# Moving one 512-token group of the shared expert across the routed-expert stage, and summing five output tiles on another engine

## The chip, the cores and the metric

The kernel runs on one core of a Trainium2 chip. The metric is device time in microseconds (us) of one execution; less is better. Five engines work side by side, each through its own list of instructions in the order in which they are written: TensorE (PE in the profile; PEld is its weight loading), VectorE (DVE), ScalarE (ACT), GpSimd (POOL) and SyncE (SP), which here issues most of the transfers. They wait for each other through semaphores. SBUF is the on-chip memory, PSUM the eight banks (128 partitions x 512 floats) that TensorE writes its results to.

## What is computed

An attention-like block, then a mixture of experts with a shared expert, over 4096 tokens of 256 numbers in float32. The part that matters here:

```
xf = layernorm(x)                                  # 4096 tokens x 256
weights, indices = top_k(softmax(xf @ Wg), 4)      # 4 of 32 experts for each token
y = sum over the 4 experts e of a token:  (silu(xg @ W1[e]) * (xg @ W3[e])) @ W2[e] * weight
z = (silu(xf @ Ws1) * (xf @ Ws3)) @ Ws2            # the shared expert, 256 wide inside
out = x + y + z
```

## The kernel before

The 4096 tokens are 32 output tiles of 128 tokens (`NT`), and for the shared expert 8 groups of 512 (`NG`), four tiles each (`QT`). The work stands in four stages.

**Attention and routing** (to about 205 us). A loop `pipelined(NT, 7, step)` per tile; at its end the normalised tokens stand transposed in `x2T_all`, and POOL has written each token's row four times, once for each of its experts, to the table `xs` in HBM (L471).

**The first shared groups** (to about 255 us). For a group g, `shared_half(g, m, n)` (L740 to L746) multiplies one half m of the shared weights, n = 0 for Ws1 and n = 1 for Ws3, into one PSUM bank `h_bank(g, m, n)`: two multiplications of 128x512. `half_silu(g, m)` (ACT, L628) writes silu of the n = 0 bank to `sg`, `half_gate(g, m)` (DVE, L1237) multiplies it with the n = 1 bank to `gsh`, and `shared_z(g)` (L753 to L760) makes from `gsh` the group's four tiles of z in turn in the banks pQV and pO, each of which `add_z(t)` (DVE, L1247) adds to the output tile `xall[:, t]`. A tile's multiplication waits until the `add_z` two tiles earlier is through. Groups 0 to 2 (`NPRE = 3`) are made here, while the last rows of `xs` are written.

**The expert stage** (about 256 to 508 us). 144 blocks of table rows (`NJ`), 128 of one expert and 16 "mixed" ones of two halves. SP loads a block (L389, L394) into one of eight `xg` buffers; `expert_step` on PE transposes it into pT0 or pQV (L947), multiplies with W1 and W3 into pS0 or pS1 (L960 to L965), transposes the gated result into pT1 or pO (L952, L970) and multiplies with W2 into pS2 or pS3 (L978 to L981). ACT copies the transposed block (L649), takes silu (L653) and writes the weighted result (L661, L666); DVE gates and copies (L1342, L1346, and L1350 for the second halves of mixed blocks); POOL scatters the result to `ys` in HBM (L499), one row for each token and expert. The blocks are staggered: in one step PE transposes block i, multiplies block i-1 and so on, and a mixed block's later parts come a step later.

**The closing stage** (508 us to the end). Once all scatters have landed, SP loads for each output tile t its four parts (128 x 4 x 256, 512 KB, L402 and L405) into one of 24 buffers `parts(t)`, the first 24 at once, the others as buffers come free, and then stores the finished tiles (L412), two at a time and the last four alone. For each tile POOL adds parts 2 and 3 to parts 0 and 1 (one 128x512 addition in SBUF, L504); ACT copies the 512 sums to a PSUM bank (`copy_parts`, L676); DVE adds the two halves to `xall[:, t]` (`add_parts`, L1258 and L1260, one operand in SBUF and one in PSUM). Beside that, the shared groups 3 to 7 are made: PE makes group g's four halves, then the z of group g-1. The order on ACT and DVE is written out by hand, tile by tile (from L694 on ACT, from `half_gate(3, 0)` on DVE): for instance `half_gate(5, 1)` stands behind `add_parts(10)`, and `add_z(12)` behind `add_parts(2)` and `half_gate(4, 1)`.

What the steps below call a half is one call of `shared_half`; the profile shows each of its two multiplications as two rows, four in all.

## Time and profile before

| | us |
|---|---|
| median of 3 runs | 570.58 (570.04 to 571.71) |
| profiled execution, its own time | 570.52 |
| its span, first to last instruction | 568.8 |
| attention and routing | 0 to 205 |
| first shared groups | 205 to 255 |
| expert stage | 256 to 508 |
| closing stage | 508 to 568.8 |

| engine | busy, share of the span |
|---|---|
| PE | 540.5 us, 95% |
| ACT | 367.4 us, 65% |
| DVE | 360.4 us, 63% |
| POOL | 331.8 us, 58% |

All times in the profile are counted from the start of the span. A busy share is a mean over stages with different limits: in the closing stage PE, POOL and the transfers are all nearly always busy, and it is the order of the waits that tells which of them the others wait for.

### The profile page before, as it was taken

Reading aid. Unit: us, or ns where it says so; the run is one execution under the profiler, and the core shown is the slowest. Engines: PE = TensorE matmul, PEld = TensorE weight load, DVE = VectorE, ACT = ScalarE, POOL = GpSimd, SP = SyncE. Lnnn points to the kernel's source line nnn. Section 1 sums busy time; section 2 is a strip of 40 time slices with the busy share of each in tenths; the row PEclk is TensorE's granted clock in tenths of the full one; section 3 lists DMA queues with packets and bytes.
Section 4 is the critical chain, followed back from the end, with each engine's and each line's share of the span. In section 5 each row is a group of like instructions: output and inputs, shape, how many; then the busy total and the mean of one; then the engine's idle time right before and its main releaser. Section 6 shows DMA issues by size and latency. Waiting matters only on the chain.

```text
span 568.8 us, 17659 instructions
## 1 busy us (share of the span) xinstructions
PE 540.5 (95%) x4793; PEld 375.6 (66%) x4793; DVE 360.4 (63%) x1353; ACT 367.4 (65%) x1258; POOL 331.8 (58%) x367
## 2 busy tenths in 40 slices
PE   6899999999999998798999999999999999979996
PEld 3465666666666664366888888888888885534554
DVE  7698999999999994751333333333333336843886
ACT  3687999898999974303666666666666665643452
POOL 6010477677777777751655565565566564447991
PEclk8999999999999999797999999999999999979999
DMA  8998365555565545935777766666666654419997
GB/s 243 318 292 292 115 224 205 203 217 200 201 228 197 213 181 188 361 115 142 221 212 216 216 199 180 187 186 171 189 184 180 181 181 144 142 67 398 409 406 265
DMA packets 65085, 123.26 MB, mean 217 GB/s; under 512 B 9824, under 2 KB 44000, under 8 KB 64992
## 3 DMA queue, kind: packets, MB, share of 16 engines
q1 hardware_dynamic: 47824, 78.07, 43.5%
q0 software_dynamic: 13056, 39.86, 19.1%
q10 hardware_dynamic: 4112, 4.19, 2.2%
q8 instruction: 45, 0.74, 0.6%
q14 instruction: 48, 0.39, 0.2%
HBM read 58.49 MB, written 63.60 MB: 215 GB/s over the span
## 4 chain that ended last, share of the span: by engine, by line
PE 79%; issue 4%; POOL 4%; DVE 4%; SPq 3%; DMA 2%; ACT 2%; ACTq 1%; POOLq 0%; DVEq 0%
PE pS L965 20%; PE pQV L830 10%; PE pS L981 9%; PE pS L743 8%; PE pS L797 5%; PE pO L890 5%; POOL xs L471 4%; PE pQV L947 3%; PE pO L871 3%; PE pT L947 2%; PE pT L776 2%; PE pO L805 2%; SPq L389 2%; DMA xg<-xs 1%; PE pQV L759 1%
## 5 line engine op out<-in xcount | busy, mean ns | idle before, releaser
L499 POOL DMA_INDIRECT ys<-gsh,dst x144 | 138.1, 959 | 118.8 <-ACT gsh L666 99.6
L471 POOL DMA_INDIRECT xs<-xg,posi x128 | 123.8, 967 | 52.1 <-issue 31.4
L965 PE MATMUL pS<-w,after_a 128*128 x512 | 134.1, 385 | 0.0
L965 PEld LDWEIGHTS pS<-w,after_a 128*128 128x128 f32 x512 | 88.4, 193 | 7.3
L981 PE MATMUL pS<-w,after_a 128*128 x256 | 76.6, 381 | 0.0
L665 ACT CAST dst<-xg 128x1 int32 x128 | 24.5, 191 | 76.8 <-PE pS L981 75.0
L1077 DVE TENSOR_TENSOR w<-pS,tri 128x512 f32<-128x512 f32 x96 | 64.9, 677 | 1.4 <-PE pS L797 1.4
L830 PE MATMUL pQV<-w 128*128 128x512 f32 x128 | 63.3, 617 | 0.5 <-ACT w L537 0.5
L1342 DVE COPY after_a<-pT 128x128 f32<-128x128 f32 x72 | 21.0, 292 | 67.3 <-PE pT L970 67.1
L1342 DVE COPY after_a<-pO 128x128 f32<-128x128 f32 x72 | 21.0, 292 | 66.6 <-PE pO L970 65.9
L666 ACT ACTIVATE gsh<-pS,xg 128x256 f32<-128x256 f32 x128 | 60.7, 474 | 0.2 <-issue 0.2
L743 PE MATMUL pS<-x2T_all,ws 128*128 128x512 f32 x112 | 54.6, 641 | 2.4 <-ACT gsh L661 1.7
L1346 DVE TENSOR_TENSOR after_a<-after_a,pS 128x128 f32<-128x128 f32 x144 | 41.4, 287 | 15.0 <-ACT after_a L653 13.7
L486 POOL TENSOR_SCALAR_AFFINE_SELECT w<-w 128x512 f32<-128x512 f32 x32 | 20.6, 644 | 42.6 <-ACT w L531 42.3
L981 PEld LDWEIGHTS pS<-w,after_a 128*128 128x128 f32 x256 | 38.7, 191 | 9.9 <-issue 0.4
L653 ACT ACTIVATE after_a<-pS 128x128 f32<-128x128 f32 x144 | 41.5, 288 | 5.0 <-PE pS L965 3.2
L504 POOL TENSOR_TENSOR w<-w 128x512 f32<-128x512 f32 x32 | 40.5, 1271 | 7.1 <-DMA w<-ys 6.9
L743 PEld LDWEIGHTS pS<-x2T_all,ws 128*128 128x128 f32 x112 | 22.6, 206 | 28.8 <-issue 26.5
L560 ACT ACTIVATE w<-pT,mwq 128x128 f32<-128x128 f32 x128 | 36.9, 380 | 1.9 <-PE pT L819 1.7
L797 PE MATMUL pS<-w 32*128 32x256 f32 x512 | 36.7, 400 | 0.0
L890 PE MATMUL pO<-w 128*32 128x128 f32 x1024 | 34.6, 274 | 2.0 <-issue 1.3
L830 PEld LDWEIGHTS pQV<-w 128*128 128x128 f32 x128 | 21.8, 190 | 19.6 <-issue 17.4
(222 smaller groups left out, 1096.0 us busy)
## 6 DMA issues: line engine op xcount, KB each, us to landing
xg<-xs SPq DMA_DIRECT2D x128, 160.0 KB, 2.5
ys<-gsh SPq DMA_DIRECT2D x32, 512.0 KB
w<-ys SPq DMA_DIRECT2D x32, 512.0 KB, 15.2
w<-in_L_ffn_W ACTq DMA_DIRECT2D x1, 4096.0 KB
out<-xall SPq DMA_DIRECT2D x14, 256.0 KB, 6.3
xs<-padrow SPq DMA_DIRECT2D x32, 80.0 KB
xg<-xs SPq DMA_DIRECT2D x32, 80.0 KB, 2.2
ys<-gsh,dst POOLq DMA_INDIRECT x144
```

The lines of the kernel that those rows point to most:

```text
L471: pool.indirect_dma_start(out=xs, out_offset=bass.IndirectOffsetOnAxis(ap=posi[:, a.r8, k:k + 1], axis=0), in_=xr[:, a.r8, :], in_offset=N ...
L499: pool.indirect_dma_start(out=ys, out_offset=bass.IndirectOffsetOnAxis(ap=dst[:, j % 8:j % 8 + 1], axis=0), in_=y[:, j % 8, :], in_offset= ...
L653: act.activation(sge[:, a.b, :], pS[a.b][:, 0:F], ACT.Silu).then_inc(S["sge_done"], 1)
L666: act.activation(y[:, a.r8, :], pS[2 + a.b][:, 0:D], ACT.Copy, scale=xg[:, a.r8, bass.ds(e + D, 1)]).then_inc(S["y_done"], 1)
L743: last = pe.matmul(h_bank(g, m, n)[:], ws13[:, k, n, m * P:(m + 1) * P], x2T_all[:, k, g * TG:(g + 1) * TG], start=(k == 0), stop=(k == KC ...
L797: last = pe.matmul(pS[j][:, g * 256:(g + 1) * 256], xnT[32 * j:32 * j + 32, a.r3, g, :], qm[32 * j:32 * j + 32, :, g, :], start=(g == 0), ...
L830: last = pe.matmul(pQV[:], xnT[:, a.r3, k, :], wqv[:, k, :], start=(k == 0), stop=(k == KC - 1))
L890: last = pe.matmul(pO[32 * j:32 * j + 32, g * P:(g + 1) * P], vp[:, a.b, 4 * g + j, r:r + 2, :], s_sb[:, j, g, r, :], start=False, stop=(r ...
L965: last = pe.matmul(pS[a.b][:, 0:2 * F], xgT[:, a.b, k, :], w13_of(e, k), start=(k == 0), stop=(k == KC - 1))
L981: last = pe.matmul(pS[2 + a.b][:, 0:D], geT[:, a.b, :], w2_of(e), start=True, stop=True)
L1077: dve.tensor_tensor(s_sb[:, j].rearrange("p g r l -> p (g r) l"), pS[j][:].rearrange("p (n l) -> p n l", l=P), tri[:].unsqueeze(1).to_broa ...
L1342: dve.tensor_copy(geT[:, a.b, :], (pT1, pO)[a.b][:, 0:P]).then_inc(S["gT_done"], 1)
```

## The change

Five edits, all about the shared groups 3 and 4 and about who sums the parts.

- Group 3's four halves are taken out of the closing stage. `shared_half(3, 0, 0)` (pS2) stands ahead of the first block of the expert stage; `shared_half(3, 0, 1)` (pS3) behind that block's transposes. The other two stand near the stage's end, `shared_half(3, 1, 0)` (pT0) and `shared_half(3, 1, 1)` (pQV), each ahead of a transpose of one of the last two mixed blocks.
- `half_silu(3, 0)` stands in ACT's second step of the expert stage; DVE multiplies in place, in `sg`, before its first step (semaphore `kept`), and only copies `sg` to `gsh` in the closing stage. The first two W2 multiplications of the expert stage wait until pS2 and pS3 are read.
- In the closing stage PE begins with group 4's four halves, in pS0 to pS3, with no wait between them, and then makes the z of group 3.
- Tiles 10, 14, 18, 22 and 26 (`ALONE`) are left out of POOL's and ACT's lists. For these DVE waits for the loaded parts, adds parts 2 and 3 to parts 0 and 1 itself (128x512, all in SBUF), and adds the two halves to `xall` from SBUF.
- Counts of the semaphores `parts_sum` and `parts_copied` are shifted accordingly (`pooled(t)`).

PE at the start of the expert stage, before, from the last z of group 2 (L759) on; `head_mask` here holds the table of block numbers, and L947 is the transpose of a block:

```order
605 L759 MATMUL pQV<-ws2,gsh 128x256 x2
606 L759 MATMUL pO<-ws2,gsh 128x256 x2
607 L943 TENSOR_LOAD head_mask
608 L947 MATMUL pT0<-ident,xg 128x128 x2
609 L943 TENSOR_LOAD head_mask
610 L947 MATMUL pQV<-ident,xg 128x128 x2
```

and in the changed kernel (L747 is a half's pair of multiplications, L951 the transpose):

```order
606 L763 MATMUL pO<-ws2,gsh 128x256 x2
607 L747 MATMUL pS2<-x2T_all,ws13 128x512 x2
608 L947 TENSOR_LOAD head_mask
609 L951 MATMUL pT0<-ident,xg 128x128 x2
610 L747 MATMUL pS3<-x2T_all,ws13 128x512 x2
611 L947 TENSOR_LOAD head_mask
612 L951 MATMUL pQV<-ident,xg 128x128 x2
```

One half stands ahead of block 0's transposes, one between them and block 1's.

PE at the end of the expert stage, before (L952 transposes the gated result of a mixed block, L978 and L979 are its W2 multiplications, L743 a half's pair):

```order
1939 L979 MATMUL pS2<-x2T_all,after_a 64x256
1940 L952 MATMUL pT1<-ident,after_a 128x128
1941 L978 ISA
1942 L978 MATMUL pS3<-w2,after_a 64x256
1943 L979 MATMUL pS3<-x2T_all,after_a 64x256
1944 L952 MATMUL pO<-ident,after_a 128x128
1945 L978 ISA
1946 L978 MATMUL pS2<-w2,after_a 64x256
1947 L979 MATMUL pS2<-x2T_all,after_a 64x256
1948 L978 ISA
1949 L978 MATMUL pS3<-w2,after_a 64x256
1950 L979 MATMUL pS3<-x2T_all,after_a 64x256
```

and in the changed kernel (L963 the transpose, L993 and L994 the W2 multiplications):

```order
1941 L994 MATMUL pS2<-x2T_all,after_a 64x256
1942 L747 MATMUL pT0<-x2T_all,ws13 128x512 x2
1943 L963 MATMUL pT1<-ident,after_a 128x128
1944 L993 ISA
1945 L993 MATMUL pS3<-w2,after_a 64x256
1946 L994 MATMUL pS3<-x2T_all,after_a 64x256
1947 L747 MATMUL pQV<-x2T_all,ws13 128x512 x2
1948 L963 MATMUL pO<-ident,after_a 128x128
1949 L993 ISA
1950 L993 MATMUL pS2<-w2,after_a 64x256
1951 L994 MATMUL pS2<-x2T_all,after_a 64x256
```

Each of the two halves now stands ahead of a transpose that the last blocks need.

DVE in the closing stage of the changed kernel, from the additions of tile 9 (L1285, L1287) over tile 10 (L1277, then L1285 and L1287 with both operands in SBUF) to the gate of group 5 (L1257) and the first z of group 4 (L1267):

```order
1315 L1285 TENSOR_TENSOR xall<-xall,pT1 128x256
1316 L1287 TENSOR_TENSOR xall<-xall,pT1 128x256
1317 L1277 TENSOR_TENSOR w13<-w13 128x512
1318 L1285 TENSOR_TENSOR xall<-xall,w13 128x256
1319 L1287 TENSOR_TENSOR xall<-xall,w13 128x256
1320 L1257 TENSOR_TENSOR gsh<-sg,pS3 128x512
1321 L1267 TENSOR_TENSOR xall<-xall,pQV 128x256
```

Before, tile 10 had two additions from pT0 in this place, and POOL and ACT had one instruction each for it.

The diff, without the shifted counts' definitions in the list of names:

```
+    ALONE = (10, 14, 18, 22, 26)
+
+    def pooled(t):
+        return t - sum(a < t for a in ALONE)
...
-                 (2, 1, 0): pS[3], (2, 1, 1): pT1}
+                 (2, 1, 0): pS[3], (2, 1, 1): pT1, (3, 0, 0): pS[2], (3, 0, 1): pS[3],
+                 (3, 1, 0): pT0, (3, 1, 1): pQV}
...
-            for t in range(NT):
+            for t in [t for t in range(NT) if t not in ALONE]:
                 pool.wait_ge(parts_in[t % PB], 16 * (t // PB + 1))
                 pool.tensor_tensor(parts(t)[:, 0:2, :], parts(t)[:, 0:2, :], parts(t)[:, 2:4, :], ALU.add
                                    ).then_inc(S["parts_sum"], 1)
...
             def expert_step(tile_of):
                 if (a := tile_of(0)) is not None:
+                    if a.t == 1:
+                        half_silu(NPRE, 0)
                     wait(act, S["xT_ps"], a.t + 1)
...
             def copy_parts(t):
-                wait(act, S["parts_sum"], t + 1)
+                wait(act, S["parts_sum"], pooled(t) + 1)
+                if t == 0:
+                    act.wait_ge(S["silu_done"], FC * NPRE + 2)
...
-            half_silu(3, 0)
             half_silu(3, 1)
...
                     last.then_inc(S["xT_ps"], 1)
+                    if a.t == 0:
+                        shared_half(NPRE, 0, 1)
                 if (a := tile_of(3)) is not None and mixed(a.t):
+                    if a.t == NJ - 2:
+                        pe.wait_ge(S["xT_done"], NJ)
+                        shared_half(NPRE, 1, 0)
+                    if a.t == NJ - 1:
+                        shared_half(NPRE, 1, 1)
                     wait(pe, S["ge_done"], a.t + 1)
...
+                    if a.t == 0:
+                        pe.wait_ge(S["silu_done"], FC * NPRE + 1)
+                    if a.t == 1:
+                        pe.wait_ge(S["kept"], 1)
                     if mixed(a.t):
...
+            shared_half(NPRE, 0, 0)
             pipelined(NJ, 4, expert_step)

             pe.wait_ge(S["y_done"], NJ)
             pe.wait_ge(S["y2_done"], NM)
             pe.wait_ge(S["gT_done"], NJ)
-            for g in range(NPRE, NG):
+            shared_half(NPRE + 1, 0, 0)
+            shared_half(NPRE + 1, 0, 1)
+            shared_half(NPRE + 1, 1, 0)
+            shared_half(NPRE + 1, 1, 1)
+            shared_z(NPRE)
+            for g in range(NPRE + 2, NG):
                 for m in range(FC):
                     shared_h(g, m)
-                if g > NPRE:
-                    shared_z(g - 1)
+                shared_z(g - 1)
             shared_z(NG - 1)
...
             def add_parts(t):
-                wait(dve, S["parts_copied"], t + 1)
+                if t in ALONE:
+                    dve.wait_ge(parts_in[t % PB], 16 * (t // PB + 1))
+                    dve.tensor_tensor(parts(t)[:, 0:2, :], parts(t)[:, 0:2, :], parts(t)[:, 2:4, :], ALU.add).then_inc(S["pair_sum"], 1)
+                    dve.wait_ge(S["pair_sum"], t - pooled(t) + 1)
+                    first, second = parts(t)[:, 0, :], parts(t)[:, 1, :]
+                else:
+                    wait(dve, S["parts_copied"], pooled(t) + 1)
+                    first, second = parts_bank(t)[:, 0:D], parts_bank(t)[:, D:2 * D]
...
-                dve.tensor_tensor(xall[:, t, :], xall[:, t, :], parts_bank(t)[:, 0:D], ALU.add).then_inc(S["half_sum"], 1)
+                dve.tensor_tensor(xall[:, t, :], xall[:, t, :], first, ALU.add).then_inc(S["half_sum"], 1)
                 wait(dve, S["half_sum"], t + 1)
-                dve.tensor_tensor(xall[:, t, :], xall[:, t, :], parts_bank(t)[:, D:2 * D], ALU.add).then_inc(S["added"], 1)
+                dve.tensor_tensor(xall[:, t, :], xall[:, t, :], second, ALU.add).then_inc(S["added"], 1)
...
+            dve.wait_ge(S["silu_done"], FC * NPRE + 1)
+            dve.tensor_tensor(sg[:, 0, :], sg[:, 0, :], h_bank(NPRE, 0, 1)[:], ALU.mult).then_inc(S["kept"], 1)
...
-            half_gate(3, 0)
+            dve.wait_ge(S["kept"], 1)
+            dve.tensor_copy(gsh[:, NPRE % 2, 0, :], sg[:, 0, :]).then_inc(S["gsh_done"], 1)
             half_gate(3, 1)
```

ACT's `copy_parts` of tiles 10, 14, 18, 22 and 26 are removed as well.

## Rows read from the trace of the kernel before

**Rows 1.** Stretches: length, busy PE, PEld, DVE, ACT, POOL, clock, DMA share, GB/s.

```profile
525.00:530.00 5.00, 4.99 (x19) 3.13 (x18) 4.38 (x12) 2.09 (x4) 4.96 (x5) 1.00 1.03 411
...
560.00:565.00 5.00, 3.81 (x16) 2.37 (x14) 4.55 (x12) 0.00 (x0) 0.00 (x0) 1.00 0.81 281
565.00:569.00 4.00, 0.00 (x0) 0.00 (x0) 0.47 (x2) 0.00 (x0) 0.00 (x0) 0.82 0.23 70
```

**Rows 2.** Timeline, POOL's and PE's closing work: start, length, instruction, idle before it.

```profile
514.09 2.52 POOL L504 TENSOR_TENSOR w<-w 128x512 f32<-128x512 f32 x2 [5.11 <-DMA w<-ys]
...
517.53 6.34 POOL L504 TENSOR_TENSOR w<-w 128x512 f32<-128x512 f32 x5 [0.92 <-DMA w<-ys]
...
524.74 31.92 POOL L504 TENSOR_TENSOR w<-w 128x512 f32<-128x512 f32 x25 [0.87 <-DMA w<-ys]
...
526.02 1.13 PE L759 MATMUL pQV<-ws,gsh 128*128 128x256 f32 x4
```

**Rows 3.** Groups by line in the closing stage: count, busy us and mean ns.

```profile
L504 POOL TENSOR_TENSOR w<-w 128x512 f32<-128x512 f32 x32 | 40.5, 1271 | 7.1 <-DMA w<-ys 6.9
...
L676 ACT COPY pT<-w 128x512 f32<-128x512 f32 x28 | 16.1, 590 | 10.1 <-DVE xall L1260 8.7 <-POOL w L504 1.4
```

**Rows 4.** Chain of waits, one half in the first shared groups: start, length.

```profile
217.21 1.72 PE pS L743 x4
```

**Rows 5.** Timeline around the start of the expert stage, DVE and PE.

```profile
254.74 0.42 DVE L1247 TENSOR_TENSOR xall<-xall,pO 128x256 f32<-128x256 f32 x1 [0.44 <-PE pO L759]
...
256.69 0.51 PE L947 MATMUL pT<-ident,xg 128*128 128x128 f32 x2 [1.99 <-DMA xg<-xs]
...
258.80 0.69 PE L947 MATMUL pQV<-ident,xg 128*128 128x128 f32 x2 [1.60 <-DMA xg<-xs]
259.28 1.91 PE L965 MATMUL pS<-w,after_a 128*128 x4
...
263.79 1.03 PE L965 MATMUL pS<-w,after_a 128*128 x4
```

**Rows 6.** Busy time by stretch around the start of the expert stage.

```profile
256.90:263.70 6.80, 5.20 (x17) 3.74 (x16) 0.36 (x2) 1.67 (x5) 0.00 (x0) 0.50 0.49 134
```

**Rows 7.** Timeline of the last blocks of the expert stage, PE, ACT and SP.

```profile
501.58 0.38 PE L979 MATMUL pS<-x2T_all,after_a 128*64 128x256 f32 x1
...
505.60 0.38 PE L979 MATMUL pS<-x2T_all,after_a 128*64 128x256 f32 x1
506.01 0.47 ACT L661 ACTIVATE gsh<-pS,xg 64x256 f32<-64x256 f32 x1
...
507.19 0.47 ACT L661 ACTIVATE gsh<-pS,xg 64x256 f32<-64x256 f32 x1
507.71 3.78 PE L743 MATMUL pS<-x2T_all,ws 128*128 128x512 f32 x4 [1.73 <-ACT gsh L661]
```

**Rows 8.** Timeline, DVE's additions and gates in the closing stage.

```profile
524.95 0.69 DVE L1237 TENSOR_TENSOR gsh<-sg,pS 128x512 f32<-128x512 f32 x1 [1.18 <-ACT sg L628]
525.55 0.41 DVE L1247 TENSOR_TENSOR xall<-xall,pQV 128x256 f32<-128x256 f32 x1
...
529.17 0.41 DVE L1258 TENSOR_TENSOR xall<-xall,pT 128x256 f32<-128x256 f32 x1
...
529.97 0.42 DVE L1258 TENSOR_TENSOR xall<-xall,pT 128x256 f32<-128x256 f32 x1
...
556.75 0.69 DVE L1237 TENSOR_TENSOR gsh<-sg,pS 128x512 f32<-128x512 f32 x1 [0.38 <-ACT sg L628]
...
565.15 0.42 DVE L1247 TENSOR_TENSOR xall<-xall,pO 128x256 f32<-128x256 f32 x1
```

**Rows 9.** Timeline in the attention stage, POOL beside a small DVE addition.

```profile
59.04 0.64 POOL L486 TENSOR_SCALAR_AFFINE_SELECT w<-w 128x512 f32<-128x512 f32 x1 [5.48 <-ACT w L531]
...
59.33 0.37 DVE L1106 TENSOR_TENSOR mcum<-mcum,mask 128x32 f16<-128x32 f16 x1
```

**Rows 10.** One line's durations: ns min/median/max.

```profile
L1106 DVE TENSOR_TENSOR mcum<-mcum,mask x16: 163/168/371, 59.3 to 229.1; 128x32 f16<-128x32 f16 x16
```

7 lines of the change are left out of this document (1 added, 6 removed).

## The prediction

> **What bounds the kernel now.** I read the stretches first, then the timelines of both ends of the expert stage and of the closing stage, because the change touches only these. The stretches of the closing stage show three resources full at once: from 525 to 530 us PE is busy 4.99 of 5 us, POOL 4.96, and the DMA engines' share is 1.03 at 411 GB/s [rows 1]. POOL works through its last 25 tiles without a pause, 1.271 us each, and ends at 556.66 [rows 2, 3]; it takes the last part at 555.4. Three times before that it stood idle for a part to land (6.9 us), the last time 0.87 us at 524.74, so the parts arrive no faster than about POOL's pace [rows 2, 3]. DVE is the engine that ends the kernel: from the last gate at 556.75 to its last addition at 565.57 it has one instruction behind the other, and 3.2 us later, with the last store, the span ends at 568.8 [rows 8]. In this tail the DMA engines have room again, 281 GB/s and then 70 [rows 1]. All that PE, POOL or the loads gain counts only as far as DVE can follow.
>
> My sum is made in the profiled execution's time, 570.52 us, which is 1.7 us more than its span and 0.06 us from the median of 570.58.
>
> **Group 3's halves leave the closing stage.** A half is four rows in 1.72 us [rows 4], so PE is rid of 4 x 1.72 = 6.9 us there, between the last expert block and the first z. But the first z tiles wait for DVE: the third tile of group 3 waits for `add_z(12)`, which stands behind `add_parts(2)` and `half_gate(4, 1)`. POOL has the sums of tiles 0 and 1 at 516.6; it starts tile 2 at 517.53, when that part has landed, and has it at 518.8. ACT's copy (0.59), two hand-overs of 0.2, two additions (0.8), a gate (0.6), `add_z` (0.42) and a hand-over give 521.9 for the third z tile, against 526.02 before [rows 2, 3, 8]. That is 4.1 us earlier instead of 6.9. It shrinks again further on, since gates 5 to 7 stand behind DVE's additions of parts that land when they land. Between 0 and 4.1 us I take 2.2 for the whole stage, about the middle: **-2.2 us**, before the ports (below) are counted.
>
> **Two halves at the start of the expert stage.** PE is free at 254.7, but waits for `add_z(11)`, 255.16; the first half then runs into the wait for block 0's load, which ended at 256.69, and delays the transposes by some 0.4 us. The second lies in the gap of 1.60 us ahead of block 1's transposes at 258.80 [rows 5] and is 0.1 us longer. Against that stands the clock: it was granted at 0.50 (1.2 GHz) from 256.90 to 263.70, after PE had idled 2 us [rows 6, 5], and block 0's four rows took 1.91 us where the same took 1.03 at 263.79. If the halves keep the clock at 2.4 GHz, two such groups give back up to 1.8 us, of which the loads' pace leaves less than all. I take **-0.6 us**; the ends are -1.8 and, if both halves run at 1.2 GHz, 2 x 3.44 - 1.99 - 1.60 = +3.3. ACT's silu (0.60) and DVE's multiplication (0.69) fall into idle time there: DVE has 0.36 us of work in 6.8 us [rows 6].
>
> **Two halves at the end of it.** Here the last blocks are a chain from PE over DVE and ACT to POOL's scatter, on which SP's loads of the parts wait, and with them the whole closing stage. The first half begins when block 140's W2 multiplication is issued, at 501.8 [rows 7], and holds block 142's transpose back until 503.5; block 141's W2 multiplication follows, then the second half until 506.3, block 143's transpose (0.33), DVE's copy (0.29) and two hand-overs, and block 143's W2 multiplication at 507.3, ending at 507.9 instead of 505.98. ACT's result stood 1.68 us behind PE's end before (507.66 - 505.98), and 1.18 us behind the block before it; with block 142 also late, at 508.9, it comes at 510.1. So the last scatter and the loads start 2.5 us later: **+2.5 us**. The bounds are 0, if PE's idle time there covered both, and 3.4, both halves in full; the walk lies nearer to the latter. The loads start later by d = -0.6 + 2.5 = **+1.9 us**, and all of the closing stage with them.
>
> **Five tiles on DVE.** POOL loses 5 x 1.27 = 6.4 us and ACT 5 x 0.59 = 3.0 us. That is worth little, since POOL goes at the pace of the parts. DVE gets a 128x512 addition for each, 0.69 us as the gate of that size [rows 8], 0.7 with its wait, 3.5 us in all; the two further additions cost as much as before. What the trace of before never shows is DVE adding two large SBUF operands while POOL reads SBUF. The nearest row is small: `mcum` (both inputs in SBUF) began at 59.33 while POOL ran from 59.04 to 59.68, and took 0.371 us instead of the usual 0.168, ending 0.02 us behind POOL [rows 9, 10]. DVE stood still until POOL was through. The bounds per tile are therefore 0 (no wait) and about 3.8 (three full POOL additions). I take: the first of the three DVE instructions waits half a POOL addition on the mean, 0.64; meanwhile POOL's next one is due, gets in behind it, and the second and third wait a whole one less the hop, 1.23 each. That is 3.1 us a tile, nearest to what the row shows, for the four tiles up to 22; when DVE reaches tile 26 POOL should be done. **12.4 us** of DVE time.
>
> The Trainium skill ("SBUF — State Buffer", section Who interferes with whom) states the same as a rule: a VectorE instruction with two SBUF inputs contends with a GpSimd instruction that reads SBUF, and whoever comes first keeps the ports for its whole instruction. By that rule the waits above are due in full; by the row alone only the wait for a running POOL instruction is certain, not that POOL gets in again between DVE's three. The row agrees as far as it goes; no row shows POOL's TENSOR_TENSOR in that place.
>
> **The sum.** DVE's list from `add_parts(0)` on, one behind the other: it can start at 514.09 + 1.27 + 0.59 and two hops, 516.4, plus d = 518.3. 32 pairs of additions at 0.79 (529.17 to 529.97) are 25.3; 20 `add_z` at 0.42 are 8.4; 8 gates at 0.60 (524.95 to 525.55) are 4.8 [rows 8]; the five extra additions 3.5; the waits at the ports 12.4; idle in the tail 0.9, as before (8.8 us from 556.75 to 565.57, of which one gate, eight `add_z` and five pairs are 7.9). The last addition ends at 518.3 + 25.3 + 8.4 + 4.8 + 3.5 + 12.4 + 0.9 = 573.6, the span at 576.8, and the execution takes **578.5 us**, 8 us more. DVE has become the bound; PE and POOL wait or are done.
>
> **Rivals.**
> - *The ports are handed over once a tile* (0.18). If POOL lets all three DVE instructions through, a tile costs the first wait alone, 0.64 us: 570.52 - 2.2 + 1.9 + 5 x 0.64 = **573.4**. For it: POOL's additions follow one another only as parts land, so its next may not be due. Against: parts land at POOL's own pace, with nothing to spare.
> - *No wait at the ports* (0.25). The one row is a 32-column instruction beside another kind of POOL instruction. Then DVE's list alone would end at 560.3, the gates and parts decide again, and the time is 570.52 - 2.2 + 1.9 = **570.2**: the gain of the closing stage is eaten at the end of the expert stage.
> - *Faster* (0.13). The ports don't matter, and PE's idle time in the last blocks (1.73 us ahead of its next half [rows 7], and more before) covers the halves there. The place is block 143's result: if it comes less than 1.1 us later than before, d is under 0.5, and 570.52 - 2.2 + d is below 568.8. With d = 0 it is **568.3**; with the clock regained at the start in full it may reach 567. For it: the transposes of the last blocks waited for others anyway. Against: the two halves stand ahead of exactly these transposes.
> - *POOL starves DVE* (0.02). If POOL keeps the ports as long as it has parts, DVE waits for its end, beyond 582.
>
> The forecast has 0.42, with a range of its own of 574 to 582: d from 0.5 to 4, and waits of 2.3 to 3.8 us a tile.
>
> **How the numbers follow.** About 0.3%, 1.7 us, is what a measurement of this kernel can tell from no change. Slower by more than that, above 572.3: the forecast 0.42, the single hand-over 0.14, the starving 0.02, and from no wait 0.03 with a large d, 0.61. Within: 0.18 of no wait, 0.04 of the single hand-over, 0.22. Faster: the faster rival 0.13 and the rest of no wait, 0.17. The range of 8 in 10 goes from 569.0, which leaves out most of the faster rival, to 581.5.
>
> **What would show it.** Right: DVE's additions of tiles 10, 14, 18 and 22 last far over 0.69 and 0.42 us, and end where a POOL addition ends; POOL's row is no longer one unbroken run; DVE's last gate comes behind 560. The last block's result comes 2.5 us later, counted from the last load of the stage; the clock around 257 to 264 stays at 1.0. Wrong: a 0.7 us addition beside POOL, which takes 12.4 us off at once, or loads of the parts that start no later than 510.5.

## The result, and the profile after

The changed kernel takes 579.62 us, the median of its six runs, beside 572.73 us for the kernel before in the same series: a ratio of 1.0126, with an interval of 1.0095 to 1.0156. It is slower by 1.3%. One of the six runs took 1860.13 us and is left out of the ratio. The profiled execution took 578.44 us (span 576.6), 7.9 us more than before's; 578.5 was forecast. The total came as forecast, but two of its pieces are off by 2.7 and 2.9 us in opposite directions. So the pieces come first.

All pieces are lengths between the same events in the two traces:

| us | before | after | difference | forecast |
|---|---|---|---|---|
| start of the span to block 143's transposes | 498.26 | 499.55 | +1.3 | -0.6 |
| from there to the end of the last block's result on ACT | 9.40 | 11.66 | +2.3 | +2.5 |
| from there to the first load of a part | 2.88 | 3.87 | +1.0 | 0 |
| first load to DVE's last gate | 46.21 | 50.52 | +4.3 | |
| last gate to the end of the span | 12.03 | 10.96 | -1.1 | |
| first load to the end, the two together | 58.24 | 61.48 | +3.2 | +6.1 |

The stretches that answer to [rows 1] and [rows 6], of the changed kernel (length, busy PE, PEld, DVE, ACT, POOL, clock, DMA share, GB/s):

```profile
257.00:264.00 7.00, 6.79 (x30) 4.28 (x29) 1.68 (x6) 2.81 (x8) 0.00 (x0) 1.00 0.47 131
...
525.00:530.00 5.00, 4.94 (x10) 3.49 (x11) 2.60 (x8) 1.18 (x2) 4.95 (x5) 0.50 1.03 414
560.00:565.00 5.00, 3.52 (x13) 2.00 (x11) 4.86 (x10) 2.30 (x4) 0.93 (x1) 1.00 1.09 384
```

At 257 to 264 us PE is now busy 6.8 of 7 us and the clock stays at full speed, where it was at half. From 525 to 530 it is the other way round: PE looks as busy as in [rows 1], but in 10 rows instead of 19, each twice as long, since the clock is at 0.50 (1.2 GHz) there. At 560 to 565 DVE is the engine without a gap, and POOL has ended at 560.93.

The timelines of POOL and of PE in the closing stage answer to [rows 2] (start, length, instruction, idle before it):

```profile
518.70 12.80 POOL L510 TENSOR_TENSOR w<-w 128x512 f32<-128x512 f32 x10 [6.05 <-DMA w<-ys]
532.79 1.27 POOL L510 TENSOR_TENSOR w<-w 128x512 f32<-128x512 f32 x1 [1.30 <-DMA w<-ys]
534.29 3.07 POOL L510 TENSOR_TENSOR w<-w 128x512 f32<-128x512 f32 x2 [0.23 <-DMA w<-ys]
538.66 3.83 POOL L510 TENSOR_TENSOR w<-w 128x512 f32<-128x512 f32 x3 [1.30 <-DMA w<-ys]
543.79 4.15 POOL L510 TENSOR_TENSOR w<-w 128x512 f32<-128x512 f32 x3 [1.29 <-DMA w<-ys]
548.90 4.17 POOL L510 TENSOR_TENSOR w<-w 128x512 f32<-128x512 f32 x3 [0.96 <-DMA w<-ys]
554.03 6.90 POOL L510 TENSOR_TENSOR w<-w 128x512 f32<-128x512 f32 x5 [0.95 <-DMA w<-ys]
```
```profile
525.06 2.07 PE L763 MATMUL pQV<-ws,gsh 128*128 128x256 f32 x4 [4.94 <-DVE xall L1267]
526.93 1.91 PE L763 MATMUL pO<-ws,gsh 128*128 128x256 f32 x4
```

POOL's one run of 25 tiles is broken wherever a tile is left to DVE: it then waits 0.95 to 1.30 us for the next part. So the five tiles save POOL nothing, as it goes at the pace of the parts (45.9 us from the first load to the end of its last addition, 46.1 before). PE stands still for 4.94 us until DVE has done `add_z(12)`, and then goes on at half the clock: a tile's z takes 2.07 and 1.91 us instead of 1.03.

And DVE's instructions for four of the five tiles (L1277 adds the pair, L1285 and L1287 add the halves), which answer to [rows 8]:

```profile
535.55 0.68 DVE L1277 TENSOR_TENSOR w<-w 128x512 f32<-128x512 f32 x1
536.27 1.37 DVE L1285 TENSOR_TENSOR xall<-xall,w 128x256 f32<-128x256 f32 x1
537.67 0.42 DVE L1287 TENSOR_TENSOR xall<-xall,w 128x256 f32<-128x256 f32 x1
...
543.02 0.68 DVE L1277 TENSOR_TENSOR w<-w 128x512 f32<-128x512 f32 x1
543.74 0.42 DVE L1285 TENSOR_TENSOR xall<-xall,w 128x256 f32<-128x256 f32 x1
544.20 1.37 DVE L1287 TENSOR_TENSOR xall<-xall,w 128x256 f32<-128x256 f32 x1
...
556.87 1.52 DVE L1277 TENSOR_TENSOR w<-w 128x512 f32<-128x512 f32 x1
558.43 1.37 DVE L1285 TENSOR_TENSOR xall<-xall,w 128x256 f32<-128x256 f32 x1
559.84 1.37 DVE L1287 TENSOR_TENSOR xall<-xall,w 128x256 f32<-128x256 f32 x1
...
564.08 0.68 DVE L1277 TENSOR_TENSOR w<-w 128x512 f32<-128x512 f32 x1
564.80 0.43 DVE L1285 TENSOR_TENSOR xall<-xall,w 128x256 f32<-128x256 f32 x1
565.26 0.42 DVE L1287 TENSOR_TENSOR xall<-xall,w 128x256 f32<-128x256 f32 x1
```

An addition of 256 columns takes 0.42 or 1.37 us. Put beside POOL's rows, the long ones are those that meet a running POOL addition: 536.27 begins in POOL's run from 534.29 to 537.36, 537.67 stands behind it; 564.08 and what follows lie behind POOL's last tile. All six of 1.37 us end 0.28 or 0.29 us behind the end of a POOL addition (537.64 against 537.36, 561.21 against 560.93). Such a wait is no idle time in the profile; it stands inside the instruction's duration, so DVE looks busy in it. There are seven: six of 0.95 (1.37 - 0.42) and one of 0.84 (1.52 - 0.68), 6.5 us in all. POOL waits as well: its addition that starts at 535.57, when DVE's of 535.55 has just begun, takes 1.79 us instead of 1.27.

### The profile page after: what moved, and what is told of

It reads as the page before. It is cut to its first block, busy times and chain, and to the rows that moved or that the text cites. A ratio compares the mean times of both kernels' runs of the same rounds, so it can differ in the third digit from the quotient of the medians.

```text
span 576.6 us, 17651 instructions
## 1 busy us (share of the span) xinstructions
PE 538.5 (93%) x4793; PEld 374.0 (65%) x4793; DVE 370.0 (64%) x1359; ACT 365.8 (63%) x1253; POOL 327.7 (57%) x362
## 4 chain that ended last, share of the span: by engine, by line
PE 66%; DVE 8%; SPq 7%; issue 7%; POOL 5%; DMA 5%; ACT 1%; ACTq 0%; DVEq 0%; POOLq 0%
PE pS L976 15%; PE pQV L834 9%; PE pS L996 8%; PE pS L801 5%; PE pO L894 5%; POOL xs L477 3%; DMA xg<-xs 3%; PE pO L875 3%; PE pT L951 2%; PE pQV L951 2%; PE pS L747 2%; DVE xall L1285 2%; PE pT L780 2%; PE pO L809 2%; SPq L379 1%
## 5 line engine op out<-in xcount | busy, mean ns | idle before, releaser
L747 PE MATMUL pS<-x2T_all,ws 128*128 128x512 f32 x104 | 50.9, 638 | 3.5 <-ACT gsh L669 2.3
L510 POOL TENSOR_TENSOR w<-w 128x512 f32<-128x512 f32 x27 | 36.0, 1342 | 12.3 <-DMA w<-ys 12.1
L747 PEld LDWEIGHTS pS<-x2T_all,ws 128*128 128x128 f32 x104 | 20.8, 206 | 27.1 <-issue 24.1
```

What stands on the lines that cost most here:

```text
L747: last = pe.matmul(h_bank(g, m, n)[:], ws13[:, k, n, m * P:(m + 1) * P], x2T_all[:, k, g * TG:(g + 1) * TG], start=(k == 0), stop=(k == KC ...
```

## The experiments

Each kernel was timed beside the kernel before on the same chip. The chips are not alike: where e5 to e7 and e8 to e10 ran, every kernel, the one before too, takes 676 to 695 us, and the clock falls again and again in the attention stage. Of those six only ratios, and lengths within a later stage, are compared. Each length is from one profiled execution. Between block 0 and block 143 of the expert stage, where the edits touch the first blocks only, the kernels on the quicker chips took 240.2 to 242.8 us (e11 244.6), so a single total says little below 2 us, and I go by lengths within a stage.

**e1: the halves are moved, DVE sums no tile alone.**

```
-    ALONE = (10, 14, 18, 22, 26)
+    ALONE = ()
```

ACT's `copy_parts` of the five tiles are back in their places.

> Only the halves of group 3 are moved; POOL and ACT sum all 32 tiles again. Theory (the ports): in the changed kernel six DVE additions of 256 columns lasted 1.37 us instead of 0.42 and one of 512 columns 1.52 instead of 0.68, 6.5 us in all, with 3.5 us of extra additions; without them the kernel takes about 571 to 573, no more than 2 us from the kernel before. Rival (the moved halves are the cause: they delayed the loads of the parts by 4.5 us): it stays at 576 or more. In either case the first load of the parts should be issued 2.5 to 4.5 us later than before, and PE should still stand idle for about 4 us ahead of the third z tile of group 3.

It took 573.66 us, ratio 1.0042 (1.0009 to 1.0074), a little over the 571 to 573 expected. From the first load to the last gate it needs 42.51 us, 3.7 less than before, and to the end 55.39, 2.9 less. What comes ahead of the first load is the same as in the changed kernel: 11.66 us from block 143's transposes to the result, and 3.73 to the load. So the closing stage gives 2.9 us by this count, and the way to it takes more. POOL is nearly one run again:

```profile
523.03 16.90 POOL L510 TENSOR_TENSOR w<-w 128x512 f32<-128x512 f32 x13 [0.15 <-DMA w<-ys]
540.58 22.97 POOL L510 TENSOR_TENSOR w<-w 128x512 f32<-128x512 f32 x18 [0.65 <-DMA w<-ys]
```

The 2.9 us are counted from a first load that comes 0.9 us later behind the last block's result than before. From the end of that result to the end of the span it is 59.12 us instead of 61.12: 2.0 less. And e12 below, whose closing stage is that of the kernel before, needs 59.91 us for it, so one trace against one trace gives between 0.8 and 2.0 us. A part of the gain is lost on PE, which waits for `add_z(12)` here too, with the clock at 0.50 from 528.17 to 531.58 us:

```profile
528.16 2.08 PE L768 MATMUL pQV<-ws,gsh 128*128 128x256 f32 x4 [3.23 <-DVE xall L1272]
```

On the chain that ended last this z tile and the next take 3.67 us, where they took 1.99 in the kernel before, and all of PE's later work stands behind them: the low clock costs 1.7 us here.

**e2: DVE sums the five tiles, the halves stay where they were.** The kernel before with `ALONE`, `pooled` and the new `add_parts`.

```
-            for t in range(NT):
+            for t in [t for t in range(NT) if t not in ALONE]:
                 pool.wait_ge(parts_in[t % PB], 16 * (t // PB + 1))
```

> Only the five tiles are summed on DVE; the halves of group 3 stand where they stood before. Theory (the ports): 573 to 577, since PE's halves in the closing stage leave DVE a little idle time that takes up part of the 6.5 us of waits and 3.5 us of additions; DVE additions of about 1.37 us appear beside running POOL additions. Rival (the moved halves are the cause): 569 to 571.

It took 577.29 us (573 to 577 expected), ratio 1.0102 (1.0051 to 1.0154). The way to the first load is before's (9.41 and 2.89 us); from there to the end it is 62.65 instead of 58.24, 4.4 more. Between the kernels with the halves moved the tiles cost 61.48 - 55.39 = 6.1. The two parts of the change lose 1.0% and 0.4% alone and 1.3% together: they add up, roughly.

**e3: the changed kernel, but DVE writes the pair's sum to the tile's PSUM bank**, so that only one of its three instructions has both operands in SBUF.

```
-                    dve.tensor_tensor(parts(t)[:, 0:2, :], parts(t)[:, 0:2, :], parts(t)[:, 2:4, :], ALU.add).then_inc(S["pair_sum"], 1)
+                    dve.tensor_tensor(parts_bank(t)[:].rearrange("p (k c) -> p k c", k=2), parts(t)[:, 0:2, :], parts(t)[:, 2:4, :], ALU.add).then_inc(S["pair_sum"], 1)
...
-                    first, second = parts(t)[:, 0, :], parts(t)[:, 1, :]
+                    first, second = parts_bank(t)[:, 0:D], parts_bank(t)[:, D:2 * D]
```

> The changed kernel, but DVE writes the sum of a tile's parts to the PSUM bank pT0 that ACT would have used, so that of a tile's three DVE instructions only the first has two SBUF operands. Theory (each instruction with two SBUF operands waits for POOL's running one): the two additions of 256 columns last 0.42 us in all five tiles, the sum of 512 columns 0.68 or up to 1.5, and the kernel is 3 to 6 us faster than the changed one, near 573 to 576. Rival (DVE waits for SBUF that POOL or the transfers keep busy, whatever the operands): no change, 577 to 581.

It took 573.76 us, ratio 1.0026 (0.9988 to 1.0064). One tile of its timeline, and the group of the pair sums (count, busy us and mean ns, then idle):

```profile
532.42 1.76 DVE L1277 TENSOR_TENSOR pT<-w 128x512 f32<-128x512 f32 x1
534.21 0.42 DVE L1285 TENSOR_TENSOR xall<-xall,pT 128x256 f32<-128x256 f32 x1
534.66 0.42 DVE L1287 TENSOR_TENSOR xall<-xall,pT 128x256 f32<-128x256 f32 x1
```
```profile
L1277 DVE TENSOR_TENSOR pT<-w 128x512 f32<-128x512 f32 x5 | 6.2, 1236 | 0.0
```

All ten additions that read PSUM take 0.42. The five pair sums take 6.2 us instead of 3.4 (5 x 0.684, e4 below), so the waits are down from 6.5 to 2.8. From the first load to the end it is 56.6 us, 4.9 less than in the changed kernel. Where DVE stands beside a running POOL addition decides it, and not its work, which is the same.

**e4: the changed kernel, but POOL fills its tiles with zeros instead of adding.** All four parts of 27 tiles are set to zero and so left out of the result, and what POOL does there reads no SBUF.

```
-                pool.tensor_tensor(parts(t)[:, 0:2, :], parts(t)[:, 0:2, :], parts(t)[:, 2:4, :], ALU.add
-                                   ).then_inc(S["parts_sum"], 1)
+                pool.memset(parts(t)[:, 0:4, :], 0.0).then_inc(S["parts_sum"], 1)
```

> The changed kernel with POOL's additions replaced by a memset of the tile's four parts, so that POOL writes SBUF and reads none; the parts of 27 tiles are left out of the result. Theory (the shared interface is POOL's reading one): all fifteen DVE instructions of the five tiles last 0.68 or 0.42 us even where a memset runs beside them. Rival (any POOL access to SBUF holds DVE up): additions of 1 us or more beside a running memset remain.

One run, 572.64 us. The timeline around tile 10, then the groups of DVE's three lines:

```profile
534.76 0.69 DVE L1276 TENSOR_TENSOR w<-w 128x512 f32<-128x512 f32 x1
...
535.15 0.95 POOL L510 MEMSET w<- 128x1024 f32 x1 [0.58 <-DMA w<-ys]
...
535.48 0.42 DVE L1284 TENSOR_TENSOR xall<-xall,w 128x256 f32<-128x256 f32 x1
```
```profile
L1276 DVE TENSOR_TENSOR w<-w 128x512 f32<-128x512 f32 x5 | 3.4, 684 | 0.0
L1284 DVE TENSOR_TENSOR xall<-xall,w 128x256 f32<-128x256 f32 x5 | 2.1, 425 | 0.2
L1286 DVE TENSOR_TENSOR xall<-xall,w 128x256 f32<-128x256 f32 x5 | 2.1, 424 | 0.2
```

The addition at 535.48 runs wholly inside a POOL instruction and takes 0.42. Nine of the fifteen begin while POOL is at such a fill, and none is stretched. From the first load to the last gate it is 42.93 us, 0.4 more than in e1 and 7.6 less than in the changed kernel. So the wait is for POOL's reading, not for its being busy or writing. Some of the 7.6 may be POOL's shorter instruction (0.95 us instead of 1.27); this run can't part the two.

**e5 and e10: the changed kernel with the halves (3,1,*) behind the last block.** The same kernel twice, on two chips.

```
-                    if a.t == NJ - 2:
-                        pe.wait_ge(S["xT_done"], NJ)
-                        shared_half(NPRE, 1, 0)
-                    if a.t == NJ - 1:
-                        shared_half(NPRE, 1, 1)
...
             pipelined(NJ, 4, expert_step)
+            pe.wait_ge(S["xT_done"], NJ)
+            shared_half(NPRE, 1, 0)
+            shared_half(NPRE, 1, 1)
             pe.wait_ge(S["y_done"], NJ)
```

> The changed kernel, with group 3's last two halves behind the last expert block's multiplications, where PE waits for ACT anyway, instead of ahead of two of its transposes. Theory (a half ahead of a transpose delays the last results by its full length): from block 143's transposes to the end of ACT's result for it 9.4 us as before, instead of 11.66, and the first load of the parts 2.3 us earlier, 3 if the later landing of the last scatter goes with it; the kernel 2 to 3 us faster than the changed one, 575 to 578. Rival (ACT's chain decides there): still 11.7 us.

> The changed kernel with the halves (3,1,*) directly behind the last block's W2 multiplication, to be timed beside the kernel before on a chip where that takes some 570 us. If the price of the end halves (2.3 us in the trace of the changed kernel) is saved in full, 577 us against the changed kernel's 579; if the late landing of the last scatter takes most of it, 578 to 579. The ports' waits stay: six 256-column additions or more at 1.37 us instead of 0.42.

Ratios 1.0128 (1.0072 to 1.0183) and 1.0125 (1.0079 to 1.0171), as the changed kernel's own on another chip. And yet the price of the end halves is gone: from block 143's transposes to the result it is 9.03 us in both, 0.4 less than before and 2.6 less than in the changed kernel. A part of it is taken back behind it. From the last scatter's start to the first load of a part it is 4.41 and 3.67 us, where the changed kernel needed 3.39 and before 2.52. The closing stage, 61.83 and 63.06 us from the first load to the end instead of 61.48, takes another part. That leaves 1.3 and 0.8 us of the 2.6, about 0.2%, which ratios known to half a per cent can't show. I had not expected the late load, and nothing in my prediction speaks of it.

**e6: the changed kernel with group 3's z additions as early as they can be.**

```
             half_gate(3, 1)
+            add_z(12)
+            add_z(13)
             add_parts(0)
+            add_z(14)
             half_gate(4, 0)
+            add_z(15)
             add_parts(1)
             add_parts(2)
             half_gate(4, 1)
-            add_z(12)
-            add_z(13)
             add_parts(3)
-            add_z(14)
-            add_z(15)
```

> The changed kernel, with DVE's four z additions of group 3 ahead of and among the additions of tiles 0 and 1 instead of behind tile 2. Theory (PE idles 3 to 5 us ahead of the third z tile of group 3 and its clock falls to 1.2 GHz for 3.4 or 6.8 us there): that idle time is under 1 us and the clock stays up; PE is 3 to 5 us further at the end of group 3. But the ports and the loads set DVE's pace, so the kernel gains 0 to 2 us only, 577 to 580. Rival (PE's idle time is part of the loss): 3 us or more faster than the changed kernel.

Ratio 1.0129 (1.0074 to 1.0184), and 62.65 us from the first load to the end instead of 61.48: nothing gained that can be seen. PE's long wait has moved to the next group. In the changed kernel it stood ahead of group 3's third z tile; here it is ahead of a z tile of group 4, whose `add_z` stands behind the gates of group 5, and the clock falls there instead (the two z rows again take twice their time):

```profile
642.67 7.13 PE L747 MATMUL pS<-x2T_all,ws 128*128 128x512 f32 x16 [0.50 <-DVE gsh L1257]
...
655.92 2.08 PE L763 MATMUL pQV<-ws,gsh 128*128 128x256 f32 x4 [4.39 <-DVE xall L1267]
```

PE is ahead of DVE, and this order only chooses where it waits. What the wait with its fall of the clock costs by itself is not measured by this; in e1, where PE sets the pace behind it, it was 1.7 us.

**e7 and e8: all three edits together** (no tile alone, halves behind the last block, early z), the same kernel on two chips.

> Halves moved, the last two behind the last block, z additions early, and no tile summed on DVE: what the other runs point to. Theory: the closing stage takes 55 us from the first load of the parts to the end, as in e1_move_only, instead of 58.2 before, and the loads start when they did before: 2 to 3.5 us faster than the kernel before, ratio 0.994 to 0.997. Rival (the transfers bound the closing stage, 21 MB at 410 GB/s): no faster than before by more than 1 us.

> Group 3's halves (3,1,*) stand directly behind the last block's W2 multiplication, DVE sums no tile alone, and the z additions 12 to 15 stand as early as their z allows. This is the same kernel as the last of the series before, to be timed beside the kernel before on a chip where that takes some 570 us. Theory (only the halves ahead of the last transposes and the ports cost anything): block 143's result comes 0.4 us earlier than before counted from its load, the closing stage from its first load to the last gate is 3.7 to 4.2 us shorter than before's 46.2, so 567.5 us. Rival (what the closing stage gains is given back between the last scatter and the first load, which in that series came 1.8 us later than before): 569 to 570.5 us, with 4.3 us from the last scatter's start to the first load.

Ratios 1.0034 (1.0004 to 1.0064) and 1.0041 (1.0014 to 1.0068). Every price in my prediction but that of the two halves at the start is taken away: the last block is 0.4 us early (9.00 and 9.03), no wait at the ports, the closing stage is 2.8 and 3.1 us shorter (55.45 and 55.15). It is still no faster than before. From the last scatter's start to the first load it is 4.32 and 4.18 us, which gives back 1.7 to 1.8, as e8's rival said. My theory for e8 expected 567.5 us on a chip like the first, which I did not get.

e7's rival, that the transfers bound the closing stage, is borne out too. The end of e8's closing stage (length, busy PE, PEld, DVE, ACT, POOL, clock, DMA share, GB/s):

```profile
665.00:670.00 5.00, 2.88 (x12) 1.60 (x10) 4.13 (x11) 0.59 (x1) 0.36 (x1) 1.00 1.09 383
670.00:673.00 3.00, 0.00 (x0) 0.00 (x0) 0.00 (x0) 0.00 (x0) 0.00 (x0) 0.95 1.09 382
```

DVE's last addition ends at 669.65, and the DMA engines stay full for 3 us more with no engine at work; in [rows 1] they had room at this place. In every kernel here the packets from the first load on are 21 MB, and the times that they take add up to 54.3 to 54.6 us for each of the 16 DMA engines on the mean. e1, e7 and e8 take 55.2 to 55.5 us from the first load to the end, so they have almost nothing left to gain there, and a load that comes later is paid for in full.

The pieces don't add up to the ratios, however. From block 143's transposes to the end it is 69.26 and 68.85 us, against 70.52 in the trace of before; by this the kernel should be 1.3 to 1.7 us faster, and it is 2 to 3 us slower. The rest lies ahead of block 143 or in how much one execution differs from the next; there is no trace of the kernel before on these two chips, and it stays open. A price of the two halves at the start of the expert stage is a rival that no run excludes: e9, below, moves only these two, needs 68.18 us from block 143's transposes to the end, and is no faster than before either.

**e9: e8 with the halves behind PE's wait for the last result.**

```
-            pe.wait_ge(S["xT_done"], NJ)
-            shared_half(NPRE, 1, 0)
-            shared_half(NPRE, 1, 1)
             pe.wait_ge(S["y_done"], NJ)
             pe.wait_ge(S["y2_done"], NM)
             pe.wait_ge(S["gT_done"], NJ)
+            shared_half(NPRE, 1, 0)
+            shared_half(NPRE, 1, 1)
```

> As the kernel with all three edits, but the halves (3,1,*) stand behind PE's wait for the last block's result, so that PE idles until ACT and DVE have written it, as in the kernel before; only the halves (3,0,*) are moved to the start of the expert stage. If the halves' activity beside the last results and their scatters is what makes the last scatter land late, the first load is issued 2.5 us behind the last scatter's start, as before, and not 4.3. If that is not it, it stays at 3.3 or more. For the start of the stage it tells the price of two halves alone: I expect blocks 3 to 10 about 1 us earlier than before and nothing left of it by block 20. In all 568.5 us in the first case, 570 in the second.

Ratio 1.0019 (0.9992 to 1.0047). The first load comes 2.50 us behind the last scatter's start, as before. This looked like an effect of PE's or ACT's activity. The DMA view says something else. It shows the queues' packets in a stretch (packets, MB, share of the 16 DMA engines). First e8, then e9, both from 0.2 to 2.5 us behind the last scatter's start:

```profile
DMA packets 95, 0.28 MB, mean 121 GB/s; under 512 B 31, under 2 KB 31, under 8 KB 93
...
q0 software_dynamic: 93, 0.25, 30.9%
q8 instruction: 1, 0.02, 4.0%
q14 instruction: 1, 0.01, 1.2%
```
```profile
DMA packets 97, 0.27 MB, mean 118 GB/s; under 512 B 32, under 2 KB 32, under 8 KB 96
...
q0 software_dynamic: 96, 0.26, 32.0%
q14 instruction: 1, 0.01, 1.0%
```

q0 carries the scatter in 96 packets. In e9 all 96 are served in that stretch; in e8 three are not, and there is a packet of another queue, q8, whose kind is "instruction". It has 16 KB (0.74 MB in 45 packets over the whole kernel before), against 0.26 MB in the 96 packets of the scatter, and occupies one of the 16 DMA engines for 0.9 to 1.7 us. The packets themselves show what it does. In e8, 93 of the 96 are through 2.05 us behind the scatter's start, as all 96 are in e9; the instruction packet runs from 1.45 to 2.92, and the last three follow right behind it, at 2.91, 3.31 and 3.60. In e5 it runs from 2.20 to 3.12, and the last three begin at 3.11, 3.53 and 3.83. I went through the traces for the last scatter:

| kernel | q8 packet behind the scatter's start | last landing | first load |
|---|---|---|---|
| before | none (next at 14.4) | 2.41 | 2.52 |
| e2 | none | 2.44 | 2.55 |
| e9 | none (next at 8.1) | 2.40 | 2.50 |
| after | 0.82, took 1.27 | 3.29 | 3.39 |
| e1, e3, e4, e6 | 0.78 to 0.82, took 0.92 to 1.05 | 3.00 to 3.19 | 3.11 to 3.29 |
| e7, e8 | 1.45, took 1.65 and 1.47 | 4.22 and 4.08 | 4.32 and 4.18 |
| e10 | 1.46, took 0.93 | 3.56 | 3.67 |
| e5 | 2.20, took 0.92 | 4.31 | 4.41 |

The trace of before has 45 such packets for 11465 instructions of PE, register and semaphore ones included: one for every 255. They are PE's own program. Where in the program PE stands when the next piece is due depends on how many instructions it has gone through. Moving a group's halves, 32 instructions with their weight loads, from behind the last scatter to ahead of it brings that moment from 522 us, among the loads, to the one scatter that everything waits for.

**e11: e8 with 96 further instructions at PE's start. e12: the kernel before with 38.** They only wait for what is long there (two waits make one instruction: 192 waits in e11, 76 in e12), and shift the place in the program at which a packet is due.

```
             keep_busy(2, 512)
+            for _ in range(192):
+                pe.wait_ge(S["zeros_dve"], 1)
             pe.wait_ge(S["w_in"], 32)
```

> The kernel with all three edits, as timed twice, and 96 further instructions at PE's start that only wait for what is long there; nothing else is changed. In every run in which the last scatter landed 3.1 to 4.4 us behind its start, instead of 2.4 to 2.5, one 16 KB packet of the instruction queue q8 (taking 0.9 to 1.6 us) was served within 2.2 us of that start; in the three where it landed in time (before, tiles on DVE alone, halves behind the last result), none was. q8 brings a packet for every 256 instructions of PE. Theory (the packet holds up the last scatter on its DMA engine): shifted by 96 instructions the packet comes some 5 us earlier, the last scatter lands at 2.4 and the first load is issued at 2.5 behind its start instead of 4.2; the kernel gains 1.7 us on the unshifted one, ratio to before about 1.001 on such a chip. Rival (PE's or ACT's activity beside the scatters): the load still comes 4.2 behind, and nothing is gained.

> The kernel before with 38 further waiting instructions at PE's start. They shift the instruction packet that before is served behind 520 us, in the middle of the part loads, to the moment when PE goes on behind the last block's result, about 1 us behind the last scatter's start. Theory: the last scatter then lands 0.6 to 1.5 us later than the 2.41 of before and the first load with it; the time grows by about as much, ratio 1.001 to 1.003. The place of the packet can be worked out to some 15 instructions only; if it is not served within 2.2 us of the scatter's start, the run tells nothing on the theory, and the load stays at 2.5. Rival (the place of instruction packets has nothing to do with it): packet beside the scatter, load still at 2.5.

In e11 the packet is served 4.55 us ahead of the last scatter; the scatter lands at 2.40 and the load is issued at 2.50, where the same kernel without the 96 instructions needed 4.18. In e12 it is served 0.79 us behind the start; the scatter lands at 3.06 instead of 2.41, the load at 3.16 instead of 2.52. The timeline of e12, and its DMA view from 0.2 to 2.5 us behind the start:

```profile
509.40 0.96 POOL L499 DMA_INDIRECT ys<-gsh,dst  x1 [0.30 <-ACT gsh L661]
...
512.56 0.81 SPq L402 DMA_DIRECT2D w<-ys  x2
```
```profile
q0 software_dynamic: 96, 0.26, 31.9%
q8 instruction: 1, 0.02, 2.6%
```

That settles the cause of the late load, in both directions and with PE's activity around the scatter unchanged. The totals don't show it. e11 has a ratio of 1.0065 (1.0045 to 1.0086): the extra instructions themselves hold PE up at the start, more than I had allowed for (its first transposes of the weights begin at 13.21 us instead of 6.43, and block 0 comes 4.6 us later than in e12 on the same chip, 0.4 of which the halves at that place explain), and 1.7 us can't be read beside that. e12 has 0.9967 (0.9940 to 0.9994), faster where the theory wanted 0.1 to 0.3% slower. In its profile the way from the first load to the end is 56.4 us, 1.9 less than before's, though none of its edits stands there. The two traces say where this comes from. First the kernel before, then e12:

```profile
507.71 16.57 PE L743 MATMUL pS<-x2T_all,ws 128*128 128x512 f32 x32 [1.73 <-ACT gsh L661]
```
```profile
509.11 15.70 PE L745 MATMUL pS<-x2T_all,ws 128*128 128x512 f32 x32 [1.73 <-ACT gsh L661]
```

In both kernels PE goes on right behind the last result, without waiting for the scatter or the load, and from there to its last z it stands idle for 0.54 us in all. The load comes 0.63 us later behind PE's start in e12, which shortens the way from the load and costs nothing. The clock, at 0.50 until 512.91 in before and until 512.81 in e12, holds PE's first 32 rows up for 5.2 us there and for 3.7 here, and they take 0.87 us less. The last 0.34 us lie behind the last gate. So in the kernel before PE sets the pace of the closing stage, and a landing that is 0.6 us late costs it nothing; where the halves are moved and the stage stands at its transfers (e7 and e8), it is due in full. The landing is shown by e11 and e12, its price in a total by none of the runs.

## Why the prediction was right, and where not

**What bounds the kernel, and the sum.** On the kernel before, the prediction says that all gains count only as far as DVE can follow. In fact PE set the pace there: it had 0.54 us of idle time from 507.71 us to its last z, DVE 9.5 us between its first and its last addition. For the changed kernel the forecast lets DVE's list set the end: last addition 573.6, span 576.8. Measured: 574.4 and 576.6. DVE is the bound in the closing stage, and the last gate comes at 565.60, behind 560 as said. But the list began 2.3 us later than forecast (first addition at 520.62, not 518.3) and was 1.5 us shorter (53.8 us, not 55.3). The first is the way to the loads, the second is the closing stage, below.

**Group 3's halves leave the closing stage** (-2.2, between 0 and 4.1). About right: by e1 3.7 us from the first load to the last gate and 2.9 to the end, but 2.0 or, beside e12, 0.8 from the last block's result. The end came later behind the last gate (12.9 instead of 12.0 us), because the transfers then fill the stage, so that 0.8 is not passed on. The walk to the third z tile gave 521.9, or 526.5 with the loads as late as they came; it was 525.06. What I missed is that PE, ready from 520.1 on, then stands still for 4.94 us, and that the clock falls in that wait (at 524.3). Moving this wait away gained nothing (e6), since the next group's takes its place.

**Two halves at the start** (-0.6, between -1.8 and +3.3). The mechanism is right: the clock stays at 2.4 GHz from 257 to 264 us, block 0's transposes come 0.9 us later (0.5 of it stands there before the stage, at `add_z(11)`, so 0.4 is the half's, as forecast), and block 5's are 1.0 us earlier (265.82 instead of 266.82). But by block 20 nothing is left of it (291.60 instead of 291.39): the forecast left the loads' pace a part of the gain, and they took all of it. At block 143 the changed kernel is 1.3 us late, which lies within what the way to it varies by from kernel to kernel (497.8 to 502.7 us on the quicker chips, e11 apart).

**Two halves at the end** (+2.5, between 0 and 3.4). Right: +2.3 in the changed kernel, e1, e3, e4 and e6 (11.66 to 11.70 us from block 143's transposes to the result), and gone in all kernels that have them elsewhere (8.99 to 9.41). The loads start at 515.08, +4.55 and not +1.9: 2.3 from here, 1.3 from the stretch ahead, and 1.0 from the instruction packet, which my prediction had no term for.

**The ports** (12.4 us, between 0 and 3.8 us a tile). The rival of no wait is out, and so is the single hand-over: at tile 22 all three of DVE's instructions waited, each for a POOL addition. This is the mechanism of the forecast, shown by e3 and e4. It is mis-sized in both of its factors. I had twelve waits (three in each of four tiles) and there were seven, because POOL, having no tile 10, 14, 18 or 22 to add, stands idle 0.95 to 1.30 us for the next part: four of the five additions that did not wait began in such a gap, and the fifth, at 535.55, came in just ahead of POOL's next. And a full wait adds 0.95, not 1.23: the DVE addition ends 1.37 us after its start, hardly longer than POOL's own 1.27. So 6.5 us instead of 12.4.

The sum of the rival *handed over once a tile*, 573.4, does not follow from the forecast's own list: without waits DVE would have ended at 560.3, some 5 us ahead of the last addition that the other terms allow, and 3.2 us of waits would have been hidden in that. It should have read 570.2, as for no wait.

The Trainium skill ("SBUF — State Buffer", section Who interferes with whom) limits the conflict to a POOL instruction that reads SBUF and a VectorE instruction with two SBUF inputs. The runs agree on both sides: POOL's fill of 0.95 us stretched none of the nine such additions that began beside it (e4), and additions with one input in PSUM took 0.42 beside POOL's additions (e3).

**What was not priced.** DVE's list had more idle time than the 0.9 us allowed: it waited 1.05 and 1.28 us for z tiles made at half the clock, 0.90 for ACT's silu, and five times 0.2 to 0.4 besides. That is some 4 us more than allowed, and it takes the place of most of the 5.9 us that the ports didn't cost. Against the forecast the way to the loads was 2.7 us longer and the closing stage 2.9 us shorter. The total was right to 0.1 us by their cancelling; the verdict of slower doesn't rest on this, since either part of the change is slower alone.

## What to carry to other kernels

Giving an engine's work to a second one pays only if the first was the bound: POOL waited for the parts before and after. If the second one has both operands in SBUF, it waits inside its instructions for each POOL addition that reads SBUF, and the profile calls this busy; compare the duration of each with its usual one. Work put into a gap ahead of the last steps of a chain is paid in full when the next stage waits for that chain; of the four halves moved, the two at the expert stage's head cost nothing that can be seen at its end, the two at its end cost 2.3 us, an instruction packet that moved with them 1.0, and the closing stage gave back 0.8 to 2.0, counted from the last block's result. Before work is moved out of a stage, look at what it leaves: here PE, DVE and the transfers had bounds within a few us of each other, and the transfers alone need some 55 us.

## What the runs showed of the hardware

- PE's instructions come in packets of 16 KB over the same 16 DMA engines as the data, one for about 255 instructions, and occupy one of them for 0.9 to 1.7 us. Beside an indirect scatter this held 3 of its 96 packets up and moved the landing from 2.4 us to between 3.0 and 4.3. If all of the next stage waits for one transfer, look for such a packet in the DMA view; where it falls changes with any edit to PE's program.
- An addition of 256 columns on DVE with both inputs in SBUF takes 0.42 us alone and 1.37 beside POOL's additions of 1.27; several in a row can each wait anew, and POOL's mean goes from 1271 to 1342 ns. POOL's fill of SBUF has no such effect, and additions with one input in PSUM stay at 0.42.
- PE stood still for 4.94 us in the closing stage, and the clock stood at 1.2 GHz from 524.3 to 531.2 us; a z tile took 2.07 us instead of 1.03.
- 96 instructions that wait for what is long there held PE's next work up by 6.8 us at the kernel's start (13.21 instead of 6.43): each is 0.05 us long in the trace, but they follow one another at 0.106 us. A wait that is fulfilled is not free.
- The kernel before took 571 to 573 us on some chips and 676 or 686 us on others. In the changed kernels block 0 came at 355 to 363 us there, with 257 to 262 on the quicker chips, and the closing stage took no longer. The two kernels that were timed on both of the slower chips had the same ratios on both (1.0128 and 1.0125, 1.0034 and 1.0041); the same kernel was not timed on a quicker and a slower chip with these edits.
- The 21 MB from the first load of the closing stage on took 54.3 to 54.6 us of each of the 16 DMA engines on the mean, whatever the kernel (in e8 at 383 to 415 GB/s while they were full); none needed less than 55.0 us from the first load to the end.
